# A Perceiver block in fp32 on one core: layer norm, fold blocks and query weights moved earlier in the first phase

## The reference, cut to what matters

```python
x = x + xattn(layernorm(x), ctx, ctx, Wq, Wk, Wv, Wd)   # 32 query heads, 8 key/value heads, head size 128, rope, causal
x = x + attn(layernorm(x), ...)                         # 32 heads of 16, causal, with biases
x = x + ffn(layernorm(x), ...)                          # base matmul plus gated low-rank experts

def xattn(q, k, v, Wq, Wk, Wv, Wd):
    queries, keys, values = heads(q @ Wq.T), heads(k @ Wk.T), heads(v @ Wv.T)
    queries, keys = rope(queries), rope(keys)
    scores = causal(queries @ repeat(keys, 4).T * 128 ** -0.5)
    return (softmax(scores) @ repeat(values, 4)) @ Wd.T
```

## Time and profile before

| what | value |
|---|---|
| median of three runs | 706.79 us |
| profiled execution | 706.06 us |
| its span from first to last instruction | 704.2 us |
| granted tensor clock | 9 tenths or more in all 40 slices, mean 1.00 |
| DVE, ACT, POOL busy | 73%, 53%, 67% |
| head 0 begins (first score matmul) | 117.80 us |

### The profile page before, as it was taken

The page is one execution under the profiler, slowest core; times in us unless marked ns, Lnnn a source line. Parts: engine busy times, 40 slices in busy tenths (PEclk is TensorE's granted clock), DMA queues, the critical chain, the costliest instruction groups (busy, mean ns, idle before and its releaser), DMA issues.

```text
span 704.2 us, 12879 instructions
## 1 busy us (share of the span) xinstructions
PE 694.8 (99%) x4841; PEld 564.0 (80%) x4841; DVE 516.4 (73%) x815; ACT 373.0 (53%) x560; POOL 471.6 (67%) x360
## 2 busy tenths in 40 slices
PE   8999999899999999999999999999999999999998
PEld 6887888688888888888888888887888888887886
DVE  5566988967767767857758758748668888899734
ACT  6356665634743743753653653654246777665220
POOL 2698155877777778778777877844525799985630
PEclk9999999999999999999999999999999999999999
DMA  7645613140400311310310312200300101011003
GB/s 263 221 150 176 172 46 106 75 164 17 135 31 18 132 35 38 106 45 30 104 45 30 104 45 65 87 16 2 104 2 1 46 31 33 2 47 46 16 1 119
DMA packets 25736, 51.08 MB, mean 73 GB/s; under 512 B 2400, under 2 KB 10720, under 8 KB 25696
## 3 DMA queue, kind: packets, MB, share of 16 engines
q1 hardware_dynamic: 25696, 50.53, 21.8%
HBM read 40.04 MB, written 10.49 MB: 72 GB/s over the span
## 4 chain that ended last, share of the span: by engine, by line
PE 83%; DVE 5%; POOL 4%; DMA 3%; issue 2%; ACT 2%; SPq 1%; DVEq 0%; POOLq 0%; ACTq 0%
PE pj L1625 12%; PE pv L1712 10%; PE pj L1712 10%; PE pj L1816 9%; PE tp L1625 8%; PE sc L1681 4%; PE tp L1712 4%; PE pj L2000 3%; PE pv L1611 3%; PE sc L1866 2%; PE tp L1879 2%; PE pv L1890 2%; PE pv L1699 2%; PE tp L1688 2%; PE sc L1699 2%
## 5 line engine op out<-in xcount | busy, mean ns | idle before, releaser
L496 POOL TENSOR_TENSOR sw<-sw,cst 128x512 f32<-128x512 f32 x72 | 96.9, 1345 | 42.3 <-ACT sw L681 42.0
L520 POOL TENSOR_TENSOR sm<-sm,mx 128x512 f32<-128x512 f32 x64 | 73.0, 1147 | 29.6 <-DVE mx L1234 16.0
L525 POOL TENSOR_TENSOR sm<-sm,rz 128x512 f32<-128x512 f32 x64 | 70.7, 1120 | 27.0 <-DVE rz L1249 27.0
L502 POOL TENSOR_TENSOR qr<-t,sw 128x512 f32<-128x512 f32 x54 | 73.9, 1369 | 7.7
L1625 PE MATMUL tp<-x,w 128*128 128x512 f32 x288 | 74.5, 395 | 0.0
L805 ACT ACTIVATE sm<-sm 128x512 f32<-128x512 f32 x64 | 40.1, 633 | 53.4 <-POOL sm L520 53.1
L514 POOL TENSOR_TENSOR w<-raw,w 128x896 fp32r<-128x896 f32 x24 | 50.3, 2118 | 26.0 <-ACT w L658 26.0
L1816 PE MATMUL pj<-xh,ws 128*128 128x512 f32 x192 | 64.6, 402 | 0.2 <-ACT kb L899 0.2
L1625 PEld LDWEIGHTS tp<-x,w 128*128 128x128 f32 x288 | 53.0, 188 | 10.8
L658 ACT ACTIVATE w<-raw 128x1792 fp32r<-128x1792 f32 x15 | 25.6, 1705 | 59.7 <-DVE raw L1109 59.7
L1625 PE MATMUL pj<-xt,w 128*128 128x512 f32 x192 | 51.7, 407 | 0.0
(11 more groups left out here) (279 smaller groups left out, 1849.6 us busy)
## 6 DMA issues: line engine op xcount, KB each, us to landing
rawd<-in_w_d SPq DMA_DIRECT2D x16, 512.0 KB, 3.4
raw<-in_w_q SPq DMA_DIRECT2D x15, 512.0 KB, 3.3
kscr<-sm SPq DMA_DIRECT2D x16, 256.0 KB, 2.1
vscr<-sm SPq DMA_DIRECT2D x16, 256.0 KB, 2.6
kr<-kscr SPq DMA_DIRECT2D x8, 512.0 KB, 3.2
vv<-vscr SPq DMA_DIRECT2D x16, 256.0 KB, 3.5
raw<-in_w_v SPq DMA_DIRECT2D x4, 512.0 KB, 3.9
X<-in_x SPq DMA_DIRECT2D x4, 512.0 KB, 6.8
```

What stands on the lines that cost most here:

```text
L496: pool.tensor_tensor(bs(sw[par][:, :]), bs(sw[par][:, :]), rep(cst[:, C_SIN:C_SIN + S], HB), ALU.mult).then_inc(sin_done, 1)
L502: pool.tensor_tensor(o, bs(t1[par][:, :]), bs(sw[par][:, :]), ALU.add).then_inc(rope, 1)
L520: pool.tensor_tensor(s3, s3, per_group(mx[:, c, :], 8), ALU.subtract).then_inc(subbed, 1)
L525: pool.tensor_tensor(s3, s3, per_group(rz[:, c, :], 8), ALU.mult).then_inc(normed, 1)
```

## The change

Layer norm's transposes stand behind value tiles 2 to 5 (`LN_AT = 2`), with the statistics, powers and applications moved ahead accordingly, and use buffers `swx` in place of `cq`. The first query weights are loaded into `raw8b` right behind x and are summed, rounded and split within the key phase, as is block 0; the second pair goes to `raw8`. Only v0 to v9 stand ahead of the fourteen products and v10 to v15 behind them (`V_LATE`). The low part of weight pair 3 is made ahead of head 0. Two temporaries of the query rope move into `kr`, so `load_kr(0)` now waits for all eight ropes. The buffer `wk1` moves in memory.

```diff
 PHASE1 = [...]
-         [("v", i) for i in range(5, 12)]
-LN_AT = 3
+         [("v", i) for i in range(5, 10)]
+V_LATE = 10
+LN_AT = 2
...
-                return cq[n % 2][:, :]
+                return swx[n % 2][:, :]
...
-        t1f, swf = t1 + [pt[0], t1x], sw + swx
+        t1f = t1 + [kr[:, i * HB:(i + 1) * HB, :].rearrange("p b s -> p (b s)") for i in range(2)]
+        swf = sw + swx
...
             sp.dma_start(bthr[:, :], b_thr).then_inc(s_cols, 16)
+            load_q(0, 0, raw8b)
...
                 if ki == 12:
                     sp.wait_ge(plo_d, 7)
-                    load_q(0, 0)
+                    sp.wait_ge(wsum, 1)
+                    load_q(0, 1)
...
-            sp.wait_ge(ln_t, NT)
-            load_q(0, 1, raw8b)
             for vi in range(6, NVT):
                 spill_v(vi)
                 if vi == 7:
-                    sp.wait_ge(wlo, 2)
-                    sp.wait_ge(wsum, 6)
+                    sp.wait_ge(wlo, 4)
                     load_q(1, 0)
                 if vi == 11:
                     for i in range(2):
                         sp.wait_ge(s_ks[i], 16 * NKT // 2)
-                    sp.wait_ge(wlo, 4)
-                    load_kr(0)
-                if vi == 12:
                     sp.wait_ge(wlo, 6)
                     load_q(1, 1)
+                    sp.wait_ge(rope, Q0 + 8)
+                    load_kr(0)
...
-                if ki in (5, 7):
-                    ln_pow((ki - 5) // 2)
+                if ki in (4, 5):
+                    ln_pow(ki - 4)
...
-                if i == 5:
+                if i == 4:
                     block_hi(0)
+                    act.wait_ge(kproj, 12)
+                    w7_hi(0, 0, raw8b, None)
+                elif i == 5:
+                    block_hi(1)
+                    block_hi(2)
+                elif i == 6:
                     act.wait_ge(kproj, NKT)
-                    w7_hi(0, 0, raw8, None)
-                elif i == 6:
-                    block_hi(1)
+                    w7_hi(1, 1, raw8, None)
+                elif i == 7:
+                    block_hi(3)
                 elif i == 8:
-                    w7_hi(1, 1, raw8b, None)
-                    block_hi(2)
-                elif i == 10:
-                    block_hi(3)
-                elif i == 11:
                     block_hi(4)
...
             w7_hi(2, 0, raw8, 13)
+            v_copy(10)
+            first_swap(6, C_BANK, None, 3)
+            v_copy(11)
+            first_swap(7, T_BANK, None, 4)
             v_copy(12)
-            first_swap(6, C_BANK, None, 3)
             v_copy(13)
-            first_swap(7, T_BANK, None, 4)
+            w7_hi(3, 1, raw8, 14)
             v_copy(14)
             v_copy(15)
-            w7_hi(3, 1, raw8, 14)
...
                 t1_k(ki)
-                if ki in (3, 5):
-                    stats_half((ki - 3) // 2)
-                if ki in (3, 8, 11):
-                    piece_lo({3: 4, 8: 5, 11: 7}[ki])
-                if ki in (9, 12, 14):
-                    n = {9: 0, 12: 2, 14: 4}[ki]
+                if ki in (3, 4):
+                    stats_half(ki - 3)
+                if ki in (3, 8):
+                    piece_lo({3: 4, 8: 5}[ki])
+                if ki in (5, 9, 11, 13):
+                    n = {5: 0, 9: 2, 11: 4, 13: 6}[ki]
                     ln_apply(n)
                     ln_apply(n + 1)
-                if ki == 9:
-                    piece_lo(6)
-            w7_sum(0)
-            ln_apply(6)
-            ln_apply(7)
...
-            block_lo(0)
-            for i in range(2):
-                w7_lo(0, 0, i)
+                if ki == 6:
+                    w7_sum(0, raw8b)
+                if ki in (9, 11):
+                    piece_lo({9: 6, 11: 7}[ki])
+                if ki == 14:
+                    block_lo(0)
+                    for i in range(2):
+                        w7_lo(0, 0, i, raw8b)
             block_lo(1)
...
             first_add(6, 6)
+            first_add(7, 7)
             w7_sum(3)
-            first_add(7, 7)
+            for i in range(2):
+                w7_lo(3, 1, i)
...
-                if first:
-                    w7_lo(3, 1, 0)
...
-                    w7_lo(3, 1, 1)
...
-            for i in range(12, NVT):
+            for i in range(V_LATE, NVT):
                 v_tile(i)
```

More of the change, by code:

```diff
@@ L121, in build @@
         wv1 = sb(p1, "wv1", [P, 2, KT, 512], F32R)
-        wk = [sb(p1, f"wk{i}", [P, 2, 2 * KT, P], F32R) for i in range(2)]
+        wk0 = sb(p1, "wk0", [P, 2, 2 * KT, P], F32R)
         sb(p1, "gap_p1", [P, 3 * 1024])
+        wk1 = sb(p1, "wk1", [P, 2, 2 * KT, P], F32R)
         wv0 = sb(p1, "wv0", [P, 2, KT, 512], F32R)
@@ L129, in build @@
         p1.close()
-        wv = [wv0, wv1]
+        wv, wk = [wv0, wv1], [wk0, wk1]
         f2 = ExitStack()
@@ L136, in build @@
         f2.close()
-        f3 = ExitStack()
-        sb(f3, "gap_f3", [P, 136 * 256])
-        t1x = sb(f3, "t1x", [P, HALF])
-        f3.close()
         pcb, u2b = sm4[0], sm4[1]
@@ L1147, in first_lo, with mix @@
                                   wk[0][:, 0, k, :].bitcast(F32), ALU.subtract).then_inc(s, 1)
+            def mix(i):
+                b11, b21, b22, b12 = xblock(0, 0), xblock(1, 0), xblock(1, 1), xblock(0, 1)
+                o, p, q = ((b11, b12, b11), (b12, b12, b22), (b22, b22, b11), (b21, b21, b22))[i]
+                dve.tensor_tensor(o, p, q, ALU.subtract).then_inc(tdone, 1)
             first_lo(0, phi_a, plo_a)
@@ L1160, in _ @@
                 t1_k(ki)
-                if ki in (3, 5):
-                    stats_half((ki - 3) // 2)
-                if ki in (3, 8, 11):
-                    piece_lo({3: 4, 8: 5, 11: 7}[ki])
-                if ki in (9, 12, 14):
-                    n = {9: 0, 12: 2, 14: 4}[ki]
+                if ki in (3, 4):
[4 more added lines that the diff above has]
+                    n = {5: 0, 9: 2, 11: 4, 13: 6}[ki]
                     ln_apply(n)
                     ln_apply(n + 1)
-                if ki == 9:
-                    piece_lo(6)
-            w7_sum(0)
-            ln_apply(6)
-            ln_apply(7)
-            def mix(i):
-                b11, b21, b22, b12 = xblock(0, 0), xblock(1, 0), xblock(1, 1), xblock(0, 1)
-                o, p, q = ((b11, b12, b11), (b12, b12, b22), (b22, b22, b11), (b21, b21, b22))[i]
-                dve.tensor_tensor(o, p, q, ALU.subtract).then_inc(tdone, 1)
-            block_lo(0)
-            for i in range(2):
-                w7_lo(0, 0, i)
+                if ki == 6:
[6 more added lines that the diff above has]
+                        w7_lo(0, 0, i, raw8b)
             block_lo(1)
-            w7_sum(1, raw8b)
+            w7_sum(1)
             dve.wait_ge(ln_cp, NT)
@@ L1188, in _ @@
             for i in range(2):
-                w7_lo(1, 1, i, raw8b)
+                w7_lo(1, 1, i)
             block_lo(2)
@@ L1192, in _ @@
             mix(2)
+            block_lo(3)
             dve.wait_ge(tdone, 3)
             mix(3)
+            block_lo(4)
             w7_sum(2)
-            block_lo(3)
-            block_lo(4)
             A2, C2 = B_BANK, T_BANK
```

## The result

| | before | changed kernel |
|---|---|---|
| median, same chip | 705.58 us (704.53 to 707.06, 16 runs) | 708.52 us (707.40 to 709.74, 16 runs) |
| profiled execution (span) | 706.06 (704.2) | 707.87 (705.9) |

The ratio is 1.0042 (95% interval 1.0033 to 1.0051): slower, where I forecast 1.2 us less, and 0.1 above my range (703.0 to 708.4). Ten of the 16 runs have a mean granted clock of 1.000, with a median of 708.03; six have 0.998, with a median of 709.64. The profiled one is of the first kind.

The account below looks back on a forecast made before the run. The tensor engine, busy 694.8 of 704.2 us, was taken as the bound, with 4.8 us to win. Terms summed to -1.2 us: 704.9 profiled, plus 0.7 to the median, 705.6 us; range 703.0 to 708.4.

Parts of the forecast that it names:

- k5, felt at k9: Sixth key tile: its multiply stands behind the second statistics, so its swap frees the bank for k9 late; +0.35 us.
- second layer norm pair: Transposes of the second pair wait for scalar-engine copies behind the late seventh weight piece; +0.5 us, ends 0 and 1.5.
- disturbed pair: Layer norm applications now end ahead of their transposes, so the earlier loss at the disturbed pair goes; -1.24 us.
- first products: Seventh product waits for the first swapped query, behind k14, low weights, k15 and block 1; +1.2 us, ends 0.2 and 1.6.
- v14 behind the last swap: Value tile v14 waits for the copy of v12, now behind both late swaps; +1.3 us, ends 0.2 and 2.4.
- keys: Key load, issued after the last query rope, lands just after v15 ends; +0.2 us, ends 0 and 3.6.
- head 0: Low weights leave the vector engine's list in head 0, so its lost time returns; -3.5 us, ends -3.6 and -2.0.
- Late keys: Rival: key load lands after 7.3 us instead of 3.9, tensor engine stands 3.4 us more; 709.0 us, chance 0.12.
- Softmax of head 0 starts late: Rival: pair 3's low weights beside GpSimd delay the first mask, 1.3 us of head 0's gain lost; 706.9 us, chance 0.13.
- No new waits: Rival: the 1.24 and 3.59 us come back, new waits stay near their lower ends; 703.0 us, chance 0.24.
- The port rule in full: Rival: vector engine and GpSimd block each other wherever two-input operations moved beside a rope, +0.6 us; 706.2 us, chance 0.16.

Follow-up runs that it names:

- e12_rope: Changed kernel with GpSimd's two instructions for k13 and k14 cut to an eighth of their columns (result differs): 707.63 us, ratio 1.0023 to the kernel before.
- e3_both: Changed kernel with the copy of v12 ahead of the last query swap and rope temporaries in other buffers, so keys load early: 706.26 us, ratio 1.0009.
- e7_low_in_head: Changed kernel with only the low weights of pair 3 put back inside head 0: 711.56 us, ratio 1.0086 to the kernel before.
- e2_keys: Changed kernel with the two rope temporaries in other free buffers and the key load back at its earlier place: 709.13 us, ratio 1.0044.
- e1_copy: Changed kernel with the scalar engine's copy of v12 moved ahead of the last query swap: 707.47 us, ratio 1.0025 to the kernel before.
- e4_order: Changed kernel with block 0 and the low weights of pair 0 behind the multiply of k15 instead of ahead: 709.27 us, ratio 1.0048.
- e13_no_mask: e5_block plus earlier value copies and v5 store, third weight pair's sum moved into a vector-engine gap; pair 3's low weights ahead of first mask: 704.27 us, ratio 0.9984.
- e8_best: e5_block plus weight pair 2's sum behind two cosine multiplies, and copies of v2 and its transposes ahead of k9's swap: 709.35 us, ratio 1.0046.
- e9_mask: e5_block with the low weights of pair 3 behind the first two masks of head 0: 706.30 us, ratio 1.0006 to the kernel before.
- e6_twelve: Changed kernel with v12 copy and early keys as in e3_both, pair 3's low weights back in head 0, twelve value tiles ahead of products: 710.56 us, 1.007.
- e5_block: e3_both plus rounding of block 1 on the scalar engine ahead of the swap of k15: 705.41 us, ratio 0.9994 to the kernel before.

## Why the prediction was wrong

By its terms, as the distance of starts in the profiled execution (the timelines above; for k5 the start of k9 against that of before, 36.94 and 36.69):

| term | predicted | measured |
|---|---|---|
| k5, felt at k9 | +0.35 | +0.25 |
| second layer norm pair | +0.5 | +1.3 |
| disturbed pair | -1.24 | -1.24 |
| first products (v8, v9, seventh product) | +1.2 | +3.0 |
| v14 behind the last swap | +1.3 | +2.2 |
| keys | +0.2 | +0.2 |
| head 0 | -3.5 | -3.6 |

The terms up to the first score add to 2.3 predicted and 5.7 measured; by the first scores themselves it is 5.6. (The mark that I gave for it, 119.7, was 0.4 below my own sum: the clock times of my schedule ran that much ahead of its terms. By the terms the products begin at 87.79 - 5.44 + 0.35 + 0.5 - 1.24 = 82.0, not at 81.6.) With head 0 the forecast was -1.2 and the profiled execution shows +1.8.

**The step that failed** is "First products, +1.2". The working named the chain and its parts rightly: from block 1 to the first addition I had 14.3 us, the trace has 14.26 (76.47 to 90.73). But I let only one of the two halves of low weights be disturbed, "1.1 more for one of them", and both were (4.04 for 2.08). Besides, block 0 began at about 66.4 instead of 65.0, since the tensor engine and the layer norm applications (3.03 us for two at 62.58) were already late. Block 1 came at 76.47 instead of 72.9. Of these 3.6 us, 1.4 are the late start of block 0 and 2.0 are GpSimd's (e12_rope: 10.04 against 8.04 us from block 0 to block 1). The tensor engine itself came 1.1 late (the transposes behind v5 at 71.00, where I had v5 end at 69.9), so 2.5 us of the 3.6 had to be waited for. The same can be read at the tensor engine: from the transposes behind v5 to the end of the fourteen products pass 0.79 + 4 x 2.72 + 19.04 = 30.7 us undisturbed, 33.7 in the changed kernel (71.00 to 104.68) and 31.6 in e12 (71.43 to 103.05). So the term measured 3.0 with GpSimd beside the chain and 0.9 without, where I had 1.2 and 0.2. That "earlier waits for it are within this sum" was right: 0.78 at v8, 1.03 at v9 and 0.67 at the seventh product are 2.5 together, and in e12_rope the first two go without the third growing. The rest of the 3.0 is 0.5 of small hand-overs among value tiles and products. That I had put the term nearer its upper end, 1.6, did not help: the end itself was too low.

**v14, 2.2 instead of 1.3.** I counted the copy at E + 12.15, at its old distance from the products' end E. With E at 104.68 the last swap ended at E + 12.3 (116.99) and not E + 11.6, the copy 0.6 behind it, and v14 began at E + 13.1. "The list that leads to that swap is the same in all three engines" was right, its durations were not: the cosine multiplies of queries 2 and 3, now with their results in `kr`, took 3.09 us beside GpSimd, where they had taken 2.39 before. The rows of the changed kernel, then those of before:

```profile
100.05 3.09 DVE L1125 TENSOR_TENSOR kr<-cq,cst 128x512 f32<-128x512 f32 x2
```
```profile
102.19 0.68 DVE L1126 TENSOR_TENSOR pt<-cq,cst 128x512 f32<-128x512 f32 x1
102.79 1.79 DVE L1126 TENSOR_TENSOR t1x<-cq,cst 128x512 f32<-128x512 f32 x1
```

Both pairs begin 4.6 us ahead of E, and the 0.7 us between them is what the last swap is late by; the other 0.2 of the 0.9 is copy and hand-over. The buffer is not the cause: e3_both has the results in `pc` and `sm`, and its pair takes as long (99.72 to 102.73 from the first start to that of the next instruction, 100.05 to 103.06 in the changed kernel). What differs is GpSimd. Before, it idled for 0.29 us up to 102.31, and the first multiply fell into that gap. In the changed kernel an addition of GpSimd ran from 99.59 to 100.89 and a sine right behind it. That this is the cause is read from the traces; no run tests it.

**Second layer norm pair, 1.3 instead of 0.5.** The seventh piece was issued at 45.58, not 44.6, and rounded at 49.30; the end I gave, 1.5, holds it. The mechanism was right, its size too small.

**Right.** Head 0: 19.81 us from the first score to its first later product (123.40 to 143.21), 19.9 predicted. e7_low_in_head shows the low weights to be 3.0 of the 3.6; the other 0.6 is gone in e7 too (22.78 against 23.39), and with it the wait of 0.45 us that the transposes had for GpSimd before. The sixth key tile: DVE's multiply of k5 at 34.94 and the end of its swap at 36.85 were forecast at 35.02 and 36.95. The slot of the keys was right too: they land at about the time v15 ends, as the two expressions E + 17.9 and E + 17.7 had it. Asked for at 119.14 and landing 3.8 us later, they were there at about 122.9, ahead of the end of v15 at about 123.3. The 0.2 of the table is therefore luck: it is 0.1 that v14 took longer behind its wait and 0.1 that stood ahead of the first score before as well, and e2_keys has it without a late key load. The late load has another price, 2 us in a kernel that removes only the wait of v14 (e1_copy). I had not said that; a reader of my sum would have thought the removal of one enough.

**The rivals.** "Late keys", at 709.0, was the nearest in number to 708.52 and did not happen: the load landed after 3.8 us, not 7.3, and the tensor engine did not wait for it. "Softmax of head 0 starts late" did not either: the first mask began at 124.60, 1.2 behind the first score, and the low weights of pair 3 ahead of it took 2.10 us. "No new waits" fell with the wait of v14. The port rule in full was the nearest in mechanism, and I had priced it at 0.6 us on the forecast, a fifth of the miss. The earlier trace rows gave 2.18 for one half beside GpSimd and 2.08 for two alone; the upper end that follows is 2.3 more for both halves, and I had written 1.1. The page "SBUF — State Buffer" of the Trainium skill (section "SBUF: two separate sides") has the two engines exclude each other for a whole instruction when the vector instruction has two inputs in SBUF. The traces agree: two halves take 2.10 us without GpSimd (e12_rope) and 3.17 to 4.29 beside it, and the cosine multiplies of the keys, which have one operand in PSUM, take 0.68 to 0.69 us in all 16 places of the changed kernel, beside GpSimd too.

**The median** is 0.5 us above that of the runs at full clock. Six of 16 runs lost 1.6 us more by the clock, see below; no term of mine held this. The 0.7 us that I added to get from the profiled execution to the median went the wrong way: the three runs I had gave the kernel before 706.79, sixteen give 705.58, 0.5 below the profiled one. So the forecast of 705.6 is just what the kernel before measures, and by the difference I missed by 4.1 us (-1.2 against +2.9), of which the terms are 3.0.

## What to carry to other kernels

Work drawn forward from behind a phase lands beside the engine that was busy in it: price every vector instruction with two inputs in SBUF there at its disturbed duration, not one of them. Here block 0 and the two halves took 5.2 to 5.6 us from start to end beside GpSimd (e1, e4, e13 and the changed kernel) and 3.6 in e12. A wait found to be the bound may hide a second one of the same length; before removing it, write down when the next input would be ready (here the keys, at E + 17.9). Moving one copy one place up in the queue of an engine that idles there gave about 1 us by itself (e1_copy against the changed kernel, 708.52 to 707.47; 0.56 at full clock), and 2.3 us together with the early keys (e3_both; 1.8 at full clock). e13_no_mask, with these and the earlier copies and sums, is 1.0 us faster than before. It keeps part of the price and part of the gain: its first score comes at 119.36, 1.56 later than before, and head 0 takes 20.63 us to its first later product, where it took 23.39.

## What the runs showed of the hardware

**A wait can cost more than its length.** In e4_order v14 waits 2.01 us and begins at 117.74, as in the changed kernel (2.03, 117.75), but the first score comes at 124.99 instead of 123.40. Stretches of 112 to 126 us in e4_order (busy us of PE, PEld, DVE, ACT and POOL, then the granted clock, the DMA share and GB/s):

```profile
112.00:118.00 6.00, 3.99 (x18) 3.06 (x17) 4.17 (x5) 2.42 (x5) 1.99 (x2) 1.00 0.39 131
118.00:122.00 4.00, 4.00 (x13) 3.12 (x13) 2.14 (x4) 1.42 (x2) 0.32 (x1) 0.63 0.43 120
122.00:126.00 4.00, 4.00 (x47) 3.19 (x47) 2.09 (x2) 1.55 (x3) 0.00 (x0) 0.94 0.64 192
```

and the same in the changed kernel's profiled execution:

```profile
118.00:122.00 4.00, 4.00 (x19) 3.26 (x19) 2.14 (x4) 1.42 (x2) 0.34 (x1) 1.00 0.47 110
122.00:126.00 4.00, 4.00 (x74) 3.34 (x73) 3.46 (x5) 1.57 (x3) 0.00 (x0) 1.00 0.65 196
```

Behind the wait the engine was granted 1.2 GHz for part of the stretch: a mean of 0.63 from 118 to 122 us, and 13 matmuls against 19. It cost 1.6 us at the first score.

The same happens behind other waits of this length. In e2_keys the profiled execution ran v14 at full clock behind its 2.02 us, but had a wait of 1.98 us for ACT among the first key tiles, up to 8.09. In e8_best a wait of 1.84 us ends at 82.28. The stretches behind them, e2 first:

```profile
9.00:12.00 3.00, 3.00 (x9) 2.38 (x9) 1.76 (x3) 2.04 (x3) 0.14 (x1) 0.58 1.06 393
```
```profile
84.00:88.00 4.00, 4.00 (x14) 3.17 (x14) 3.97 (x4) 1.66 (x2) 0.00 (x0) 0.73 0.73 202
```

The profiled executions of the fifteen kernels have eleven waits of the tensor engine from 1.76 to 2.11 us. Five were followed by a stretch at half clock (e2_keys 1.98, e4_order 2.01, e8_best 1.84 and 2.11, e9_mask 1.94) and six were not (the changed kernel 2.03, e1_copy 1.95, e2_keys 2.02, e6_twelve 1.76, e7_low_in_head 1.99, e12_rope 2.06). None of the shorter ones was, the longest of 1.58 us (e4_order, v9).

The run times fit this without proving it, since only a profiled execution shows where the clock fell. A mean clock below 1.000 have 6 of 16 runs of the changed kernel, 4 of 6 of e2_keys, 4 of 6 of e4_order, 3 of 5 of e7_low_in_head and 9 of 12 of e12_rope, all with a wait of 2 us at v14. In three of them the runs fall in two groups, 1.4 to 1.6 us apart: the changed kernel at 708.03 and 709.64 us, e2_keys at 707.9 and 709.3, e12_rope at 706.2 and 707.8. e3_both, e5_block and e13_no_mask, whose longest waits from 5 us on are 0.8 to 1.1 us, have one run below 1.000 each of 12, 11 and 11. The page "TensorE: Matmul & The Clock Gate" of the Trainium skill (Part 1) says that idleness drops the engine to half clock; the five stretches agree, each behind a single wait of about 2 us. e1_copy is a loose end: it waits 1.95 us for the keys, and yet its twelve runs lie within 706.91 and 708.67, two of them at 0.999. The profiles don't say why.
